# A second routing on Trainium2: seven tiles chosen ahead of the last, places counted behind the first shared chunk, the first block's products between the last shared tiles

## What is computed

```
x = layernorm(x + mix(x))                     # a linear recurrence over tokens, then two output products
logits = x @ router_w                         # 1024 x 8
top2, idx = top_k(logits, 2); scores = softmax(top2)
combined = sum over the two chosen experts e of score * ((silu(x @ w1g[e]) * (x @ w1u[e])) @ w2[e])
shared = (silu(x @ w_gate) * (x @ w_up)) @ w_down      # inner width 1024
out = layernorm(x + combined + shared)
```

## Time and profile before

| what | us |
|---|---|
| median of 3 timed runs (lowest, highest) | 815.77 (815.47, 816.55) |
| the profiled execution, as timed | 817.82 |
| its span, first to last instruction | 815.7 |

### The profile page before, as it was taken

How to read it: one execution, slowest core, us unless ns; L and a number is a source line. 1 busy time by engine, 2 the same in 40 slices (tenths; PEclk the granted TensorE clock), 3 DMA queues, 4 the chain that set the end, 5 groups by cost and what they waited for, 6 DMA issues and landing times.

```text
span 815.7 us, 16017 instructions
## 1 busy us (share of the span) xinstructions
PE 775.1 (95%) x4629; PEld 657.7 (81%) x4629; DVE 558.0 (68%) x1425; ACT 397.6 (49%) x898; POOL 271.4 (33%) x357
## 2 busy tenths in 40 slices
PE   8999989999999999999989999899999999999997
PEld 7888867777778788777778999789897778888786
DVE  5333778787868778777746666468857377777666
ACT  1334656656656666566524444323233266666531
POOL 2004446443433333222345666615423400000071
PEclk9998999999999999999999999999999999999999
DMA  6449961000000000009239899787621335555431
GB/s 234 120 121 380 406 246 47 30 29 28 22 29 21 23 22 22 21 14 319 100 110 296 294 353 354 253 285 282 243 111 42 126 101 154 154 154 154 111 98 64
DMA packets 50097, 121.78 MB, mean 149 GB/s; under 512 B 7280, under 2 KB 17648, under 8 KB 49904
## 3 DMA queue, kind: packets, MB, share of 16 engines
q1 hardware_dynamic: 39040, 96.46, 35.8%
q0 software_dynamic: 7680, 21.51, 7.4%
q10 hardware_dynamic: 3312, 3.02, 1.1%
HBM read 77.18 MB, written 43.78 MB: 148 GB/s over the span
## 4 chain that ended last, share of the span: by engine, by line
PE 71%; DVE 10%; issue 8%; POOL 5%; DMA 4%; ACT 3%; DVEq 0%; ACTq 0%; POOLq 0%; SPq 0%
PE scores L1620 9%; PE scores L1619 9%; PE scores L1618 9%; PE scores L1843 6%; PE acc_ps L2029 5%; PE misc_ps L1749 4%; PE misc_ps L1747 4%; PE probsT_ps L1734 4%; PE probsT_ps L1756 3%; PE scores L1853 3%; PE acc_ps L1734 3%; DVE xT_lo L1089 2%; POOL xd_d L766 2%; DVE neg_max L1083 2%; PE probsT_ps L1832 2%
## 5 line engine op out<-in xcount | busy, mean ns | idle before, releaser
L815 ACT ACTIVATE area<-scores,neg_max 128x128 f32<-128x128 f32 (+7 forms) x128 | 94.9, 742 | 86.8 <-DVE neg_max L1083 86.3
L1083 DVE TENSOR_REDUCE neg_max<-scores 128x1 f32<-128x128 f32 (+7 forms) x128 | 95.8, 750 | 22.7 <-PE scores L1706 22.7
L697 POOL DMA_INDIRECT xe_d<-x_rows,send_i x64 | 64.1, 1001 | 55.4 <-ACT x_rows L839 38.5
L727 POOL DMA_INDIRECT ye_d<-area,home_i x64 | 61.1, 955 | 40.7 <-DVE home_i L1290 18.4
L1618 PE MATMUL scores<-kT_hi,weff_hi 128*128 128x512 f32 (+3 forms) x172 | 67.2, 390 | 0.6 <-ACT area L792 0.4
L1843 PE MATMUL scores<-area 128*96 128x128 f32 x512 | 66.5, 273 | 1.3 <-DVE area L1255 0.8
L685 POOL CAST weff_hi<-area 128x256 fp32r<-128x256 f32 x42 | 17.0, 406 | 136.2 <-PE scores L1706 88.5
L1620 PE MATMUL scores<-kT_hi,weff_lo 128*128 128x512 f32 (+3 forms) x172 | 62.1, 361 | 0.0
L1619 PE MATMUL scores<-kT_lo,weff_hi 128*128 128x512 f32 (+3 forms) x172 | 62.0, 361 | 0.0
L1843 PEld LDWEIGHTS scores<-area 128*96 128x96 f32 x512 | 59.2, 163 | 2.1 <-issue 1.0
L772 POOL DMA_INDIRECT area<-yd_d,slot x16 | 15.3, 954 | 135.8 <-DMA yd_d<-area 131.3
(11 more groups left out here) (290 smaller groups left out, 2049.6 us busy)
## 6 DMA issues: line engine op xcount, KB each, us to landing
area<-w SPq DMA_DIRECT2D x23, 512.0 KB, 4.0
area<-gate_up SPq DMA_DIRECT2D x24, 384.0 KB, 6.0
xe_d<-area SPq DMA_DIRECT2D x8, 1088.0 KB, 12.3
ye_d<-area SPq DMA_DIRECT2D x8, 1024.0 KB, 16.9
area<-w SPq DMA_DIRECT2D x8, 1024.0 KB, 7.3
area<-ye_d SPq DMA_DIRECT2D x15, 512.0 KB, 4.9
area<-xe_d SPq DMA_DIRECT2D x28, 272.0 KB, 6.2
area<-head_w SPq DMA_DIRECT2D x16, 448.0 KB, 3.4
```

Source lines behind the costliest of these rows:

```text
L697: pool.indirect_dma_start(xe_d, bass.IndirectOffsetOnAxis(send_i[:, t, k:k + 1], 0), x1_rows[:, t, :], None).then_inc(sent[k % 2] if t < T ...
L815: act.activation(row_of(n)[:, 0:L], score_bank(n)[:, 0:L], ACT.Exp, bias=neg_max[:, n % 4:n % 4 + 1], accum_out=rsum[:, s, k:k + 1]).then_ ...
L1083: dve.tensor_reduce(neg_max[:, n % 4:n % 4 + 1], score_bank(n)[:, 0:(n // HEADS + 1) * P], AX.X, ALU.max, negate=True).then_inc(max_ready, 1)
```

## The change

On PE the transposes of tiles 0 to 3 move ahead of the last `mix`, the others right behind it; tiles 0 to 3, then 4 to 6, are routed before tile 7 is transposed, and only tile 7 is routed behind that, into a bank of its own (`acc`). Thirteen idle products stand where there were sixteen. The counting moves from behind shared chunk 1 to behind chunk 0. The last shared tile is cut in two halves of four products, with `block_T` of block 1 and `block_in` of block 0 between them. On DVE the two best of tiles 0 to 6 are found ahead of tile 7's; its copy of a quarter of x3T is gone (ACT makes all of them, in six pieces in place of four); the splitting of x for the first half goes to POOL, one half on each side of the last inverse root; `split_weights(1)`, which shared chunk 1 waits for, moves from ahead of the routing to behind the tally; `shared_gated` and the later splits each move one step back; `add_shared(3)` moves behind the first `block_gated`. SP is unchanged.

```diff
 # POOL, ahead of the 16 indirect transfers
+            def split_first_x3(c):
+                pool.wait_ge(x3T_half, c + 1)
+                pool.tensor_tensor(x3T_lo[:, c, 0:BANK], x3T[:, c, 0:BANK], x3T_hi[:, c, 0:BANK].bitcast(f32),
+                                   ALU.subtract).then_inc(x3T_split, 1)
+
+            split_first_x3(0)
             rstd_of(rank3(TILES - 1), 1)
+            split_first_x3(1)
 # ACT
             round_weights(0)
+            act.wait_ge(lu_done, TILES)
+            act.wait_ge(r_done, TILES)
             for c in range(HC):
                 act.wait_ge(x3T_ps, c + 1)
                 act.copy(x3T[:, c, 0:BANK], half[2 * c]).then_inc(x3T_done, 1)
             act.wait_ge(x3T_done, HC)
             round_x3(0)
-            act.wait_ge(x3T_ps, 3)
-            act.copy(x3T[:, 0, BANK:], half[1]).then_inc(x3T_done, 1)
+            later = T - BANK - P
+            for c in range(HC):
+                act.wait_ge(x3T_ps, HC + c + 1)
+                act.copy(x3T[:, c, BANK:T - P], half[2 * c + 1][:, 0:later]).then_inc(x3T_done, 1)
             round_weights(1)
-            act.wait_ge(x3T_done, 2 * HC)
+            for c in range(HC):
+                act.wait_ge(x3T_ps, 2 * HC + c + 1)
+                act.copy(x3T[:, c, T - P:], half[2 * c + 1][:, later:]).then_inc(x3T_done, 1)
+            act.wait_ge(x3T_done, 3 * HC)
             round_x3(1)
 # DVE
-            dve.wait_ge(x3T_ps, 4)
-            dve.tensor_copy(x3T[:, 1, BANK:], half[3]).then_inc(x3T_done, 1)
-            split_x3(0)
-            split_weights(1)
...
+            for ready, bank, first, end in ((1, misc, 0, TILES - 1), (2, acc, TILES - 1, TILES)):
+                dve.wait_ge(lg1_ready, ready)
+                link(dve.tensor_copy(lg1[:, first:end],
+                                     bank[:, first * E1:end * E1].rearrange("p (t e) -> p t e", e=E1)))
...
             link(dve.tensor_tensor(ch1, oh1[:, :, 0, :], oh1[:, :, 1, :], ALU.add))
-            shared_gated(0, 0)
-            split_weights(2)
             for m in range(3):
...
             dve.sem_inc(ch1_done, 1)
+            split_weights(1)
             dve.wait_ge(pl1_ready, 1)
...
-            shared_gated(0, 1)
-            split_weights(3)
+            shared_gated(0, 0)
+            split_weights(2)
...
             add_shared(2)
             block_T(1, 1)
-            add_shared(3)
             chunks = w1_chunk(dve, 1)
             split_w1(1, chunks, range(HC))
             block_gated(0, 0)
             split_w1(1, chunks, range(HC, CHUNKS))
+            add_shared(3)
 # PE
             steps_two(pe, step)
-            run_idle(5)
-            mix(TILES - 1, 1)
...
+            pe.wait_ge(x3_done, 4)
+            transpose_x3(range(4))
+            run_idle(2)
+            mix(TILES - 1, 1)
             pe.wait_ge(x3_done, TILES - 1)
-            transpose_x3(range(4))
             transpose_x3(range(4, TILES - 1))
+            pe.wait_ge(ld_router1, 32)
+            pe.wait_ge(x3T_done, HC)
+            route1(range(4), misc)
+            run_idle(3, pT[0])
+            pe.wait_ge(x3T_done, 2 * HC)
+            route1(range(4, TILES - 1), misc).then_inc(lg1_ready, 1)
             run_idle(4, pT[0])
-            pe.wait_ge(ld_router1, 32)
-            route1(0)
             pe.wait_ge(x3_done, TILES)
             transpose_x3([TILES - 1])
             run_idle(4, pT[0])
-            route1(1).then_inc(lg1_ready, 1)
-            run_idle(3, pT[0])
+            pe.wait_ge(x3T_done, 3 * HC)
+            route1([TILES - 1], acc).then_inc(lg1_ready, 1)
...
             shared_in(0, 0)
-            shared_in(0, 1)
             pe.wait_ge(ch1_done, 1)
...
-            for k in range(2, SC):
+            for k in range(1, SC):
                 shared_in(0, k)
-            shared_out(0, first_rows)
+            for q in range(3):
+                shared_out(0, q)
+            block_T(0, 0)
+            shared_out(0, 3, range(SC // 2))
             block_T(1, 1)
...
             block_in(0, 0)
-            pe.wait_ge(sh_read, TILES // 2)
+            shared_out(0, 3, range(SC // 2, SC))
+            pe.wait_ge(sh_read, 3)
             block_pe(0, 0)
+            pe.wait_ge(sh_read, 4)
             block_pe(1, 1)
```

More of the change, by code:

```diff
@@ L1405, in split_weights, with split_last_x3 @@
                 ins.then_inc(shw_split, 1)
-            def split_x3(b):
+            def split_last_x3():
                 for c in range(HC):
-                    part = slice(b * BANK, (b + 1) * BANK)
-                    dve.wait_ge(x3T_half, HC * b + c + 1)
-                    dve.tensor_tensor(x3T_lo[:, c, part], x3T[:, c, part], x3T_hi[:, c, part].bitcast(f32),
+                    dve.wait_ge(x3T_half, HC + c + 1)
+                    dve.tensor_tensor(x3T_lo[:, c, BANK:], x3T[:, c, BANK:], x3T_hi[:, c, BANK:].bitcast(f32),
                                       ALU.subtract).then_inc(x3T_split, 1)
@@ L1422, in _ @@
             normalise(rank3(TILES - 1), y[:], x1[:, TILES - 1, :], 1).then_inc(x3_done, 1)
-            dve.wait_ge(x3T_ps, 4)
-            dve.tensor_copy(x3T[:, 1, BANK:], half[3]).then_inc(x3T_done, 1)
-            split_x3(0)
-            split_weights(1)
             link = chain(dve, d_step)
-            dve.wait_ge(lg1_ready, 1)
             dve.wait_ge(consts1, 6)
[L1431 to L1437, removed]
+            for ready, bank, first, end in ((1, misc, 0, TILES - 1), (2, acc, TILES - 1, TILES)):
+                dve.wait_ge(lg1_ready, ready)
+                link(dve.tensor_copy(lg1[:, first:end],
+                                     bank[:, first * E1:end * E1].rearrange("p (t e) -> p t e", e=E1)))
+                for t in range(first, end):
+                    ins = dve.max(tv1[:, t, :], lg1[:, t, :])
+                link(ins)
+                for t in range(first, end):
+                    ins = dve.max_index(ti1[:, t, :], tv1[:, t, :], lg1[:, t, :])
+                link(ins)
             dve.tensor_tensor(weight1[:, :, 0:1], tv1[:, :, 1:2], tv1[:, :, 0:1], ALU.subtract).then_inc(tanh1, 1)
@@ L1469, in _ @@
             dve.tensor_copy(slot1[:], sl1[:]).then_inc(slots1_ready, 1)
-            shared_gated(0, 2)
-            split_weights(4)
+            shared_gated(0, 1)
+            split_weights(3)
             sh6 = [P, BLOCKS, E1]
@@ L1485, in add_shared @@
                 dve.tensor_tensor(shared[:, t, :], pT[t % 2][:, 0:HID], x1[:, t, :], ALU.add).then_inc(sh_read, 1)
-            for c in range(3, SC):
+            for c in range(2, SC):
                 shared_gated(0, c)
@@ L1491, in _ @@
                 if c == 3:
[L1492 removed]
+                    split_last_x3()
             def block_gated(i, u):
@@ L1963, in shared_in, with shared_out @@
                 last.then_inc(gs_ready, 1)
[L1965 to L1968, removed]
+            def shared_out(b, q, chunks=range(SC)):
+                for k in chunks:
+                    if k == 0 and 4 * b + q >= 2:
                         pe.wait_ge(sh_read, 4 * b + q - 1)
[L1970 to L1974, removed]
+                    if q == 0:
+                        pe.wait_ge(hs_done, b * SC + k + 1)
+                    last = pe.matmul(pT[q % 2][:, 0:HID], hs[:, k, q * P:(q + 1) * P], sh_d[:, k, :],
+                                     start=k == 0, stop=k == SC - 1)
+                if k == SC - 1:
                     last.then_inc(sh_ready, 1)
@@ L2056, in _ @@
                 shared_in(1, k)
-            shared_out(1)
+            for q in range(4):
+                shared_out(1, q)
 def kernel(**inputs):
```

13 lines of the change are left out of this document (4 added, 9 removed).

## The result

Over 12 executions the changed kernel took **811.2 us** in the median (808.65 to 814.96), and the kernel before, on the same chip, 815.83 (814.65 to 818.63): ratio 0.9949, 95% interval 0.9929 to 0.9968. The forecast was 811.4, its range 809.6 to 813.5. The profiled execution took 810.46 us, its span is 808.7.

What follows compares the result with a forecast made beforehand. PE was taken to bound the kernel. Start -2.6, chunk clock -1.6, chunk waits +0.4, rows -1.16, gated result -0.97 gave -5.9; from the median, 815.77 - 2.6 order - 1.7 clock = 811.4 us, range 809.6 to 813.5.

Steps and rivals of the forecast that it cites:

- PE up to the first chunk: PE from the last `mix` to the first shared chunk: 6.77 us at full clock, the chunk 2.6 us sooner.
- Chunk clock: First products of shared chunk 0, formerly at half clock: 1.6 us fall away if the clock holds.
- Chunk waits: PE waits 0.9 us for chunk 1's weight split, perhaps 0.1 at the next two chunks; net +0.4.
- Rows: Slot ready at 617.1, 6.6 us sooner; block 0's rows usable at 641.8, before PE ends shared tile 2 at 643.4.
- Rows' wait and gated result: PE's waits for block 0's rows (1.16 us) and, behind `block_in`, for the gated result (0.97 us) both go.
- Half of the clock term against the median: Of the clock's 3.3 us, at the routing and first chunk, the middle, 1.7, was taken off the timed median.
- the price of profiling: Whole kernel: if profiling explains the 2.05 us between profiled execution and median, all 5.9 come off, giving 809.9.
- the trace does not bear it out: DVE's splits beside POOL's sends: mutual exclusion judged unsupported, as the split pair at 609.13 takes the same 0.76 us.
- the slower rival: Clock falls early in the routing and stays: first chunk 2.9 us later, 817.0 to 819.1 us; chance 0.04.
- I let the whole tail shift with it: Behind `block_hT` of block 0, PE's list is unchanged and waits short, so the whole gain reaches the end.
- The sign named for the prediction being wrong as a whole: Block stage: PE waits that it had not before would mean the shift does not reach the end.
- The first rival: Around the routing the clock falls as before, so only order is gained: 813.2 us; chance 0.20.

Runs made afterwards that it cites:

- e1: The kernel before with routing products widened from 8 to 128 columns, the 8 router columns read 16 times; 813.35 us, ratio 0.996.
- e3: The changed kernel with routing products 128 columns wide and shared tile 3 whole again ahead of `block_in`; 811.74 us, ratio 0.9948.
- e2: The changed kernel with routing products widened from 8 to 128 columns; 810.68 us, ratio 0.9928 to the kernel before.
- e10: The changed kernel once more, unchanged; 810.46 us beside 814.87 for the kernel before, ratio 0.9947.
- e9: The same kernel as e6, unchanged, on another occasion; 810.63 us from twelve executions, ratio 0.995.
- e6: Changed kernel with 128-column routing, chunk 1's weights split ahead of the logits, POOL's second subtraction behind the last normalise, 4 of 11 idle products; 806.97 us, ratio 0.9911.
- e8: e6 with the weight split that chunk 1 needs moved from DVE to POOL; 809.14 us, ratio 0.9933.
- e5: The changed kernel with POOL's second subtraction of x waiting until DVE has normalised the last tile; one execution, 811.37 us.

## Why the prediction was right, point by point

- **PE up to the first chunk.** 6.77 us predicted, 6.82 measured; gain 2.56 for 2.6. e1 divides it: 1.53 clock (11.21 less 9.68) for 1.7, 1.03 order for 0.9.
- **Chunk clock.** From the first chunk to the shared tiles e1 takes 23.00 where before took 24.60: 1.60, as predicted.
- **Chunk waits.** +0.4 predicted; after takes 23.33 against e1's 23.00, +0.33. The one wait of 0.9 is 0.51 as PE shows it, since DVE's tally came sooner: its last row ends 2.66 behind the first chunk's start, where I had 2.9.
- **Rows.** Slot ready 7.44 us behind the first chunk (615.91), 7.6 predicted. The sends pass at 1.29 us each (616.20 to 635.52, 15 gaps), a little faster than the 1.33 used. SP issues the first load at 637.93 and block loads there take 2.0 to land, so 2.2 us stay before PE's 642.16; 1.6 was predicted.
- **Rows' wait and gated result.** -1.16 and -0.97, both gone. e3 puts the second back at 0.63, not the whole 0.97.
- **The sum.** 5.9 predicted from mix to `block_hT` against the profiled execution, 6.35 measured; in it order 2.6 predicted and 2.59 measured, clock 3.3 predicted and 3.65 measured. That the two figures for order agree so well is partly luck. The rows' wait was counted whole as order, and e1 leaves 0.65 of its 1.16: the other 0.51 were the clock's. Against that, from the shared tiles to `block_hT` e2 takes 2.01 less than e1 (17.24 for 19.25), more than the 1.62 that the two waits of e1 add up to.
- **Half of the clock term against the median.** 1.7 was taken; the gain in medians, 4.6, less 2.6 of order leaves 2.0, and less the 1.3 to 2.4 of order that reach the end of the traces 2.2 to 3.3. The reason given, that the clock differs between executions, is shown by e10. The size is not: 1.7 was the middle between two ends, e1's gain by the wide routing is 2.1 in the median with 1.5 to 5.0 by the ratio's interval, and e2 shows no gain of the changed kernel's median by it. That the forecast came out so close is luck in that measure. The alternative, that 2.05 us were the price of profiling, is not borne out: the 817.82 of the profiled execution lies within the 814.65 to 818.63 of the 12 now seen, and the changed kernel's profiled execution lies 0.74 below its median. The Trainium skill (TensorE: Matmul & The Clock Gate, What's actually happening) has the word "run-variable" for the number of slow products at the start of one kernel; the two profiles of one program, 8.65 and 11.40, show the like in its middle.

What was wrong, though it moved the time little:

- The step "the trace does not bear it out" on DVE and POOL excluding each other. I weighed it for the sends alone. The pair that I named, at 609.13, had no send about and could show nothing of them; the answer was right all the same (after's five pairs of weight splits beside sends take 0.75 to 0.81). But the change puts a POOL subtraction beside DVE's normalise, and that took 1.35 for 0.41. The 2 us of cover counted for tile 7 hid it; without them it would have been a wait of 0.9.
- The price of the slower rival. It put the first chunk 2.9 us later than before and the clock's rise 3.5 us behind it. e10 had such a fall, at 604.93: the chunk came 0.19 later than before's, behind the mix, the clock rose 1.08 us into it, and the whole way was still 3.57 shorter than in the profile before. The rival's mechanism exists; its price did not.
- The step "I let the whole tail shift with it". Behind `block_hT` the kernel before and e1 take 159.26 and 159.29, the changed kernel 159.61 and 159.69, its variants 159.49 to 160.63. So 0.2 to 1.4 us of the shift do not reach the end. The sign named for the prediction being wrong as a whole, waits in the block stage that were not there, is absent in the two profiles of the changed kernel and present in five of its variants, with 0.27 to 0.66 us.
- The first rival, the clock falling as before (813.2), is no case apart: it is some of the executions, as e10's 812.78. A median lies between.

## What to carry to other kernels

Split a gain into what the order of the work gives and what the clock gives before adding it to a median: the first was in every profile here, the second only in some. One profile of each kernel cannot separate them; a version in which the thin products are widened can, as here 2.59 from 3.65. Then follow the gain to the end of the trace: of 2.59 at a mark in the middle 1.33 to 2.38 were left there. And when a step moves to another engine, look at who runs beside it at its new place, not only at who ran beside it at the old one.

## What the runs showed of the hardware that was not expected

**A wide product costs what a thin one does here.** A routing record of 128 columns takes 0.112 us from start to start (28 records in 3.13 us in e9), one of 8 columns 0.107 at full clock. e1, with the wide ones, is 2.1 us faster in the median than the kernel before.

**DVE and POOL hold each other up.** DVE's normalise, one instruction of 128x256, takes 0.41 us alone and 1.35 beside POOL's subtraction of 512 columns (603.86 to 605.14), and ends 0.14 us behind it. In e6, where the normalise is out of the way, the pair of weight splits takes the blow; rows of DVE and POOL in its timeline:

```profile
601.14 1.83 DVE L1419 TENSOR_TENSOR kT_lo<-area,kT_hi 128x256 fp32r<-128x256 f32 x2
601.30 1.38 POOL L764 TENSOR_TENSOR xT_lo<-area,xT_hi 128x512 fp32r<-128x512 f32 x1 [0.53 <-DVE x_rows L1135]
```

1.83 for 0.76, and POOL 1.38 for 1.27: it waits a little, too. In e8 POOL's two subtractions of 256 columns (606.72, 1.42 us) run beside DVE's choosing, and DVE's row there is as long as elsewhere (0.57 for seven, after has 0.58):

```profile
607.02 0.57 DVE L1450 MAX8 tv<-lg 128x8 f32<-128x8 f32 x7
```

The Trainium skill (SBUF — State Buffer, Who interferes with whom) names both kinds: a DVE instruction with two SBUF inputs, and `tensor_scalar` where it can enter a two-port mode; one with a single input otherwise stays free. The weight splits (two inputs) and the choosing (one) agree with it. For the normalise no run shows in which mode it ran: its 0.41 us are as long as the 0.42 of DVE's two-input add of the same size (601.85 in after), so the rows give no sign of a faster one. That POOL's subtraction held it up is e5's result; by which of the two kinds, no run shows.

**What stays open.** What decides whether the clock falls in a given execution of one program no row here shows. From the start of the second half's shared tiles to the end the changed kernel takes 20.07 us and the one before 19.74. These 0.3 us lie behind DVE's last instruction, from whose end to the end of the span pass 2.55 for 2.23 (2.23 again in e8); their cause was not tried.
